# One score table with a running maximum over the level in place of masked scores per group, a rebuilt prologue and new engine lists, in a one-core transformer block

## What is computed

```python
levels = _compute_levels(token_ids, NUM_LEVELS)      # scan: clip(lvl + d, 0, 31)
h = level_emb[levels] * SCALE
h = h + attn(layernorm(h))      # 16 query heads, 4 key/value heads, head size 16, softmax over the 128 keys
h = h + ffn(layernorm(h))       # ternary weights W1, W2; relu(x @ W1.T + b1) @ W2.T + b2, 1024 hidden units
# _quantize(W): gamma = mean(|W|); clip(round(W / (gamma + 1e-5)), -1, 1)
```

## Time and profile before

| what | value |
|---|---|
| median of 3 runs | 60.76 us |
| lowest and highest | 60.25 and 62.35 us |
| span of the profiled execution | 59.6 us, the only time the profile gives for it |
| mean granted TensorE clock | 0.927 |
| busy: PE, PEld, DVE, ACT, POOL | 51.9, 40.2, 46.7, 37.6, 19.0 us |

### The profile page before, as it was taken

One profiled execution on the slowest core, in us unless ns is written; L12 is line 12 of the kernel. 1 busy time (PEld: TensorE's weight loads), 2 busy tenths in 40 slices (PEclk: granted clock), 3 DMA queues, 4 the chain that ended last, 5 costly groups with the idle time before them and its releaser, 6 DMA issues.

```text
span 59.6 us, 1125 instructions
## 1 busy us (share of the span) xinstructions
PE 51.9 (87%) x358; PEld 40.2 (68%) x358; DVE 46.7 (78%) x140; ACT 37.6 (63%) x99; POOL 19.0 (32%) x30
## 2 busy tenths in 40 slices
PE   2999999999999999989769999897999999996000
PEld 0333698555476997868448899596899989994000
DVE  1899795889999667469999999999998999427500
ACT  2726429960098876995999498697767599027400
POOL 6431000499999900000940009992000000000000
PEclk9999998555589999999999999999999999999985
DMA  0469799854100000000000000000000066700694
GB/s 0 85 195 202 225 396 415 302 151 122 50 0 5 0 0 0 16 0 0 0 0 0 0 0 0 11 0 0 0 0 0 0 207 228 259 19 1 214 346 144
DMA packets 4496, 5.36 MB, mean 90 GB/s; under 512 B 986, under 2 KB 3979, under 8 KB 4491
## 3 DMA queue, kind: packets, MB, share of 16 engines
q1 hardware_dynamic: 4458, 5.28, 27.3%
q10 hardware_dynamic: 32, 0.01, 0.1%
HBM read 3.19 MB, written 2.10 MB: 89 GB/s over the span
## 4 chain that ended last, share of the span: by engine, by line
PE 60%; DVE 23%; ACT 5%; issue 4%; DVEq 1%
PE psmisc L995 12%; PE psg L818 8%; PE pswt L974 7%; DVE tern L643 4%; DVE hl L712 4%; ACT cT L442 3%; DVE xn L697 3%; PE psg L871 3%; PE psg L873 3%; PE psg L903 3%; PE psg L872 3%; PE psg L895 3%; PE psg L918 2%; DVE hq L681 2%; DVE st L685 2%
## 5 line engine op out<-in xcount | busy, mean ns | idle before, releaser
L456 ACT ACTIVATE hr<-pswt,b1c 128x256 f32<-128x256 f32 x16 | 7.5, 476 | 2.7 <-PE pswt L974 2.2
L995 PE MATMUL psmisc<-w2T,hh 128*128 128x256 f32 x32 | 8.4, 291 | 0.3 <-DVE hl L712 0.3
L995 PE MATMUL psmisc<-w2T,hl 128*128 128x256 f32 x32 | 8.1, 282 | 0.0
L712 DVE TENSOR_TENSOR hl<-hr,hh 128x256 fp32r<-128x256 f32 x16 | 7.7, 509 | 0.3
L364 POOL TENSOR_SCALAR sg<-w 128x1024 bf16<-128x1024 f32 x2 | 7.2, 3628 | 0.0
L974 PE MATMUL pswt<-xhi,w1T 128*128 128x256 f32 x32 | 7.0, 299 | 0.0
L995 PEld LDWEIGHTS psmisc<-w2T,hh 128*128 128x128 f32 x32 | 6.1, 189 | 0.7 <-DVE hl L712 0.5
L974 PE MATMUL pswt<-xlo,w1T 128*128 128x256 f32 x32 | 6.4, 280 | 0.0
L995 PEld LDWEIGHTS psmisc<-w2T,hl 128*128 128x128 f32 x32 | 6.1, 190 | 0.0
L818 PE MATMUL psg<-warm 128*128 128x512 bf16 x11 | 5.1, 629 | 1.2 <-DVE tiny L540 1.2
L643 DVE SCALAR_TENSOR_TENSOR tern<-aw,thr,sg 128x512 bf16<-128x512 f32 x8 | 5.6, 739 | 0.0
(11 more groups left out here) (152 smaller groups left out, 124.4 us busy)
## 6 DMA issues: line engine op xcount, KB each, us to landing
w<-in_L_ffn_W_dram SPq DMA_DIRECT2D x4, 512.0 KB, 6.1
out_dram<-aw SPq DMA_DIRECT2D x8, 256.0 KB, 2.6
wq<-in_L_attn_Wq_dram SPq DMA_DIRECT2D x1, 256.0 KB, 2.8
wo<-in_L_attn_Wo_dram SPq DMA_DIRECT2D x4, 64.0 KB
emb<-in_L_tok_level_emb_dram SPq DMA_DIRECT2D x1, 128.0 KB
bo_bc<-in_L_attn_bo_dram SPq DMA_DIRECT2D x1, 128.0 KB, 7.6
b_bc<-in_L_ffn_b_dram SPq DMA_DIRECT2D x1, 128.0 KB, 6.2
wk<-in_L_attn_Wk_dram SPq DMA_DIRECT2D x1, 64.0 KB, 2.0
```

Source lines behind the costliest of these rows:

```text
L456: nc.scalar.activation(hr[:, n % NHR, :], pswt[n % 2][:, 0:RH], ACT.Relu, bias=b1c[:, j:j + 1]).then_inc(a_hr, 1)
L712: V.tensor_tensor(hl[:, n, :], hr[:, n % NHR, :], hh[:, n, :].bitcast(F32), ALU.subtract).then_inc(v_hl, 1)
L995: ins = mm(psmisc[r][:, 0:D], part[:, n, r * P:(r + 1) * P], w2T[:, j, :], start=(g < HALF and j == 0 and m == 0), stop=(j == FC - 1 and m ...
```

## The change

What it does, part by part:

- Scores are made once for all sequences: `scores()` is two matmuls of 128 columns with no mask (query rows on partitions, 4 key heads by 32 levels). The levels that a sequence has are a gapless range from 0 or from 1 up to its highest. Two DVE scans (`prefix_max`) give the running maximum along the level, one starting at level 0, one at level 1; `prefix_t`, `prefix_out` transpose and copy them; `level_ends`, `end_codes`, `end_columns` find the highest and lowest level of each sequence, `top_onehot` makes a one-hot of it, and the matmuls `maxima()` pick for each sequence the running maximum at its highest level. `max_hi`, `max_parts` split it into `ms`, and one `less_max()` of 16 matmuls on 32 partitions each serves all four groups, with one semaphore for all. `neg` and its matmul, the four reductions, `mxr` and `max_t` are gone.
- The prologue is rebuilt. The token DMA brings three copies of the tokens, so that one compare each handles the three opening and the three closing brackets, and a matmul (`drops`) adds them up; the scan then reads PSUM. Queries are made on 128 output partitions (4 matmuls in place of 8), the bias matmuls go first, ACT takes the high parts of the queries, POOL makes one half of `wqh`, `xT4`, `rep` and `sel`. `warm_up` is 5, 2 and 2 in place of 10 and 1.
- The signs of W1 go from ACT to DVE (1024 elements in each of two instructions). The copies into `cT` are shared: per group two on ACT and two on DVE. `magnitudes(1, 1)` goes ahead of the exponentials, and `table_bias` ahead of `threshold(0)`.
- All four lists are in a new order.

The diff, cut to its core:

```diff
+            act.dma_start(tok3[:], x.unsqueeze(0).to_broadcast([3, B, S])).then_inc(d_tok, 16)
...
             def exps(g, b):
-                act.wait_ge(p_et, g + 1)
                 if g == 0 and b == 0:
-                    act.wait_ge(v_cpos, 2)
+                    act.wait_ge(p_et, 1)
+                    act.wait_ge(v_cpos, 1)
...
             def ctx_out(g):
                 act.wait_ge(p_cT, g + 1)
-                for c in range(2):
-                    src = psg[g][64 * c:64 * c + 64, 0:D].rearrange("p (b a e l) -> p a e b l", b=2, a=2, e=H2)
-                    for a in range(2):
-                        dst = cT[64 * a:64 * a + 64, g].rearrange("p e (b c) l -> p c e b l", c=2)
-                        nc.scalar.activation(dst[:, c], src[:, a], ACT.Copy).then_inc(a_cT, 1)
+                for a in range(2):
+                    src, dst = ctx_halves(g, 0, a)
+                    ins = nc.scalar.activation(dst, src, ACT.Copy)
+                ins.then_inc(a_cT, 1)
...
+            query_hi(0)
+            query_hi(1)
             magnitudes(0, 0)
             magnitudes(0, 1)
-            signs(0)
+            prefix_out()
             magnitudes(1, 0)
-            max_out(0)
-            signs(1)
-            max_out(1)
-            max_out(2)
+            max_hi()
+            magnitudes(1, 1)
             exps(0, 0)
...
+            dve.wait_ge(c_opc, 6)
+            V.tensor_scalar(opened[:], tok3[:], opc[:, 0:1], None, ALU.is_equal).then_inc(v_cmp, 1)
             dve.wait_ge(v_st1, 1)
...
+            V.scalar_tensor_tensor(drop[:].rearrange("b (s e) -> b s e", e=2)[:, :, 0], tok3[:], opc[:, 1:2], opened[:],
+                                   ALU.is_equal, ALU.subtract).then_inc(v_drop, 1)
...
+            def level_ends():
+                dve.wait_ge(v_lev, 1)
+                V.tensor_reduce(ends[:, 0:1], levels, AX_X, ALU.max).then_inc(v_ends, 1)
+                V.tensor_reduce(ends[:, 1:2], levels, AX_X, ALU.min).then_inc(v_ends, 1)
+
+            def end_codes():
+                dve.wait_ge(v_ends, 2)
+                for i in range(2):
+                    V.scalar_tensor_tensor(ends[:, 2 + i:3 + i], ends[:, 1:2], (64.0, -64.0)[i], ends[:, 0:1],
+                                           ALU.mult, ALU.add).then_inc(v_code, 1)
+
+            def end_columns():
+                dve.wait_ge(c_sele, 1)
+                for i in range(2):
+                    dve.wait_ge(v_code, i + 1)
+                    V.tensor_scalar(endx[:, i, :], sele[:], ends[:, 2 + i:3 + i], None, ALU.mult).then_inc(v_endx, 1)
...
+            def top_onehot(i):
+                dve.wait_ge(p_ends, 1)
+                dve.wait_ge(c_row, 1)
+                V.scalar_tensor_tensor(top[:, i, :].rearrange("p (n k) -> p n k", k=KV),
+                                       pswt[1][:, i * P:(i + 1) * P].rearrange("p (n k) -> p n k", k=KV),
+                                       pnum[:, 0:1] if i == 0 else pm64[:, 0:1], bm[:].unsqueeze(1).to_broadcast([P, P // KV, KV]),
+                                       ALU.is_equal, ALU.mult).then_inc(v_top, 1)
+
+            def prefix_max(i):
+                dve.wait_ge(p_s, 1)
+                dve.wait_ge(c_reset, 3)
+                V.tensor_tensor_scan(pmx[:, i, :], reset[:, i, :], psmisc[1][:, 0:P], ABSENT, ALU.add, ALU.max).then_inc(v_pmx, 1)
...
+            def max_parts():
+                dve.wait_ge(c_row, 2)
+                dve.wait_ge(a_mhi, 1)
+                V.scalar_tensor_tensor(ms[:], mhi[:].bitcast(F32), lowrow[:, 0:1], psmisc[1][:, 0:P], ALU.mult, ALU.add).then_inc(v_ms, 1)
+
+            def signs(i):
+                dve.wait_ge(d_w1[i], 16)
+                V.tensor_scalar(sg[:, 0, i * 1024:(i + 1) * 1024], halves(0, i), 0.0, 0.5, ALU.is_ge, ALU.subtract).then_inc(v_sgn, 1)
...
-
-            def maxima(g):
-                dve.wait_ge(p_s, g + 1)
-                V.tensor_reduce(mx[:, g, :], psg[g][:, :].rearrange("p (n l) -> p n l", l=L), AX_X, ALU.max).then_inc(v_mx, 1)
...
+            def ctx_out(g):
+                dve.wait_ge(p_cT, g + 1)
+                for a in range(2):
+                    src, dst = ctx_halves(g, 1, a)
+                    ins = V.tensor_copy(dst, src)
+                ins.then_inc(v_cT, 1)
...
+            absent()
+            values()
+            table_bias()
             threshold(0)
-            maxima_hi(3)
```

PE's side of it (its list stands above):

```diff
+            def drops():
+                pe.wait_ge(v_drop, 1)
+                pe.wait_ge(c_seld, 1)
+                mm(pswt[1][0:B, 0:2 * S], seld[:], drop[:], start=True, stop=True).then_inc(p_drop, 1)
...
-            def less_max(g):
-                pe.wait_ge(a_ms, g + 1)
-                if g == 0:
-                    pe.wait_ge(c_sel, 2)
+            def less_max():
+                pe.wait_ge(v_ms, 1)
+                pe.wait_ge(c_sel, 1)
                 for b in range(BG):
-                    ins = mm(psg[g][:, b * P:(b + 1) * P], sel4[:, b * P:(b + 1) * P], ms[:, g, :], start=False, stop=True,
-                             skip_group_check=True)
+                    for g in range(NG):
+                        q = slice(L * g, L * (g + 1))
+                        ins = mm(psg[g][:, b * P:(b + 1) * P], sel[q, b * P:(b + 1) * P], ms[q, :], start=False, stop=True,
+                                 skip_group_check=True)
```

More of the change, by code:

```diff
@@ L220, in level_tower @@
         v_klo = sem("v_klo")
[L221 to L222 removed]
+        a_qhi = sem("a_qhi")
+        v_qlo = sem("v_qlo")
         v_vo = sem("v_vo")
@@ L752, in _ @@
             normalise(1)
+            ctx_out(0)
             ternary(0, 3)
-            inverse_sums(2)
-            table_bias()
-            normalise(2)
+            ctx_out(1)
             add_table(0)
@@ L844, in _ @@
-            pe.wait_ge(a_wqh, KC)
-            for h in range(G):
-                for k in range(KC):
-                    mm(psg[3][0:64, h * L:(h + 1) * L], wqh[:, k, h], xT1[:, k, 0:L], start=(h == 0 and k == 0), stop=False,
-                       skip_group_check=True)
-            pe.wait_ge(a_bqr, 1)
-            for h in range(G):
-                ins = mm(psg[3][0:64, h * L:(h + 1) * L], bqr[:, h], ones[0:1, 0:L], start=False, stop=True, skip_group_check=True)
-            ins.then_inc(p_q, 1)
@@ new lines, in query_bias, with levels_out @@
+            def query_bias():
+                pe.wait_ge(a_bqr, 1)
+                for a in range(2):
+                    mm(psg[3][:, a * L:(a + 1) * L], bqr[:, a], ones[0:1, 0:L], start=(a == 0), stop=False, skip_group_check=True)
+            def levels_out():
+                pe.wait_ge(v_lev, 1)
+                pe.wait_ge(c_selb, 1)
+                levels = lev[:].rearrange("b (s e) -> b s e", e=2)[:, :, 1]
+                for g in range(NG):
+                    ins = mm(pswt[0][:, g * S:(g + 1) * S], selb[:, g * P:(g + 1) * P], levels, start=True, stop=True)
+                ins.then_inc(p_lev, 1)
@@ new lines, in keys, with queries @@
+            def keys():
+                pe.wait_ge(a_xT1, 1)
+                pe.wait_ge(a_wk, 1)
+                for k in range(KC):
+                    ins = mm(psmisc[1][:, 0:L], wk[:, k].rearrange("p r n -> p (r n)"), xT1[:, k, :], start=False, stop=(k == KC - 1))
+                ins.then_inc(p_k, 1)
+            def queries():
+                pe.wait_ge(a_xT1, 1)
+                pe.wait_ge(a_wqh, 1)
+                pe.wait_ge(g_wqh, 1)
+                for a in range(2):
+                    for k in range(KC):
+                        ins = mm(psg[3][:, a * L:(a + 1) * L], wqh[:, k, a, :], xT1[:, k, :], start=False, stop=(k == KC - 1),
+                                 skip_group_check=True)
+                ins.then_inc(p_q, 1)
@@ new lines, in level_ends, with values @@
+            def level_ends():
+                pe.wait_ge(v_endx, 2)
+                pe.wait_ge(c_ones, 2)
+                mm(pswt[1][:, 0:2 * P], ones16[:], endx[:].rearrange("p i n -> p (i n)"), start=True, stop=True).then_inc(p_ends, 1)
+            def values():
+                pe.wait_ge(v_oh, 2)
+                pe.wait_ge(d_bv, 16)
+                mm(pswt[0][:, 0:KVD], ones[0:1, :], bvr[:], start=True, stop=False)
+                pe.wait_ge(d_wv, 16)
+                pe.wait_ge(g_xT4, 1)
+                for k in range(KC):
+                    mm(pswt[0][:, 0:KVD], xT4[:, k].rearrange("p b l -> p (b l)"), wv[:, k, :], start=False, stop=(k == KC - 1))
@@ new lines, in prefix_t, with maxima @@
+            def prefix_t():
+                for i in range(2):
+                    pe.wait_ge(v_pmx, i + 1)
+                    ins = nc.tensor.transpose(psmisc[0][:, i * P:(i + 1) * P], pmx[:, i, :], identf[:])
+                ins.then_inc(p_pmT, 1)
+            def maxima():
+                pe.wait_ge(a_pmT, 1)
+                pe.wait_ge(v_top, 2)
+                for i in range(2):
+                    ins = mm(psmisc[1][:, 0:P], top[:, i, :], pmT[:, i, :], start=(i == 0), stop=(i == 1))
```

(20 more changed lines are left out.)

627 lines of the change are left out of this document (325 added, 302 removed).

## The result

The changed kernel takes 67.78 us (median of four executions, 67.30 to 69.10) against 60.52 for the kernel before on the same chip (60.25 to 62.35); the ratio is 1.119, 95% interval 1.107 to 1.131. The forecast was 59.5, its range ended at 62.8, and the direction is wrong as well. The profiled execution took 67.94 us, its span is 65.5.

The account below looks back on a forecast made before the run. It took DVE, handing over with ACT, to have little room after a prologue to 18.35, and PE to bound from 41.8; -0.1 - 1.0 - 1.2 + 2.1 - 1.2 = -1.4, less 0.2, gave 59.5 us against 60.76, range 57.0 to 62.8.

Parts of the forecast that it names:

- Prologue, predicted -0.1: Up to the exponentials: PE at the lower clock needs 11.3 us behind xT1, exponentials at 18.2 against 18.35.
- rival 1: Prologue: warm-ups bring the full clock by about 6 and short matmuls hold it, 57.5 us; chance 0.30.
- the limit I named for a fast prologue: Prologue: with table_bias ahead of threshold(0), DVE waits for bo_bc until 16.1; no cost in the forecast itself.
- Other things in this stage are hidden: Prologue: POOL's new copies and selectors (4.4 to about 9), DVE's identities and the bo_bc wait cost nothing.
- My last sentence on what could go wrong: Closing caveat: an untimed wait, above all POOL's sel before less_max or sg before the ternaries of W2.
- The first term: Attention: context(0) starts at 19.3 in place of 20.3, once four exponentials are through; -1.0 us.
- The second term: Attention: sharing cT copies between ACT and DVE saves 0.6 us for each of the first two groups; -1.2.
- rival 2: Attention: clock at 1.2 GHz from 18 to the first long out_proj or ffn1 run, about +3.3, 62.8 us; chance 0.23.
- The window of rival 2: Attention: a granted clock under about 0.75 in 18 to 27 us would decide for rival 2.
- Hand-over, predicted +2.1: Second to fourth x_lo: DVE's new list takes 11.1 to 11.3 us, before 9.1; fourth x_lo at 41.7.
- Rival 3: Hand-over: DVE has 1.5 us more than taken, so the gain is given back, 60.7 us; chance 0.12.
- Last stretch, predicted -1.2: Behind the fourth x_lo, PE-bound: 13 ffn2 calls stand ahead of ffn1(1, 0), before 8; five at 0.24 us.

Follow-up runs that it names:

- e1: The changed kernel plus 11 dummy matmuls where PE waits, from the exponentials to the third group; 67.29 us, ratio 1.086 to the kernel before.
- e5: e4 plus 11 dummy matmuls where PE waits in the attention; 64.15 and 64.39 us undisturbed, 65.60 median.
- e6: e5 with all four cT copies of a group on ScalarE; 64.35 and 64.45 us undisturbed, ratio 1.060.
- e10: e6 with the signs of W2 made by VectorE instead of GpSimd, ahead of threshold(0); 62.57 us, ratio 1.027.
- e13: e10 with ten warm-up matmuls in a row at the start in place of five; 61.41 us in one undisturbed execution, median 63.51.
- e15: e13 with table_bias back in the attention, one W2 sign operation earlier, no warm-ups ahead of the scores; 60.61 and 60.89 us undisturbed, median 63.29.
- e11: The kernel before with GpSimd's list as in the change, so both W2 sign operations come later; 62.71 us, ratio 1.030.
- e8: The kernel before with only the shared cT copies, two of four per group on VectorE; 61.87 and 62.31 us undisturbed, ratio 1.022.
- e12: e10 without the 11 dummy matmuls; 64.26 us, ratio 1.054.
- e4: The changed kernel up to less_max, then the old order on PE, ACT and DVE, shared cT copies kept; 66.87 us, ratio 1.091.
- e7: e1 with the order of before from the first ffn1 on, spread(1, *) side by side; 64.96 us undisturbed, 66.50 median.
- e2: The changed kernel with the four spread(1, b) calls in a row; 66.82 us median, 65.15 in one undisturbed execution.

## Why the prediction was wrong, step by step

The runs form a ladder, by undisturbed executions: the change 67.6; with the clock held (e1) 66.3; with the old order too (e5) 64.3; copies back on ScalarE (e6) 64.4; signs off GpSimd (e10) 62.6; the kernel before 61.0. That is 1.3 + 2.0 - 0.1 + 1.8 + 1.6 = 6.6 us. Most rungs come from different chips. By the ratios to the kernel before, which ran beside each (60.4 undisturbed beside the change, 61.1 beside e1), the same steps are 2.0 + 1.7 - 0.1 + 2.0 + 1.6 = 7.2, so a single step may be off by 0.3, the first by 0.7. The order in which parts are undone matters too: the signs give 1.8 in the old order, 0.8 to 1.4 on one execution in the new one. The last 1.6 is not taken apart further than by e13 and e15.

**Prologue, predicted -0.1, measured +0.9.** The clock was called right (the lower level to the end), which rules rival 1 out. Two terms were mis-sized. PE was through with the transposes of `xT1` at 6.2, where I had the copy ready at 5.8; and PE needed 12.4 us behind them, not 11.3: the four matmuls of the query bias, 0.85 us [L952 in the chain], were in no term. The 22 passes took the 5.3 us that they were priced at. `less_max` was 0.6, not 1.0. That nothing waits for `bo_bc` held, and e13 shows the limit I named for a fast prologue: DVE waits until 17.2.

**"Other things in this stage are hidden": the step that failed unseen.** It priced GpSimd's new copies and not the rest of GpSimd's list. The value copies wait for DVE's `values`, which moved 6 us back, and the first sign operation of W2 went with them; the second was moved by hand, and its new place was not priced either. My last sentence on what could go wrong named `sg` before the ternaries of W2, without a time or a chance. e10 and e11 price it at 1.7 to 1.8 us in the old order, from both sides.

**Attention, predicted -1.0 and -1.2, measured +0.2.** The first term held in part. Six exponentials take 1.66 us from 19.27, so the fourth is through at 20.4, and `context(0)` follows at 20.55: 1.3 us behind the first exponential, where it was 2.0 before. That is -0.7; it doesn't show in the start of `context(0)`, because the prologue ends late. What `abs_total(1)`, which stands ahead of it in PE's list and waits for DVE's `thr`, costs it is 0.15 at the most. My sum also books the prologue's -0.1 twice, as 19.3 already holds it. The second term, -1.2, is the one that failed: from the first `context` to the second `x_lo` it is 13.2 us where it was 12.3. The copies were costed by what they take from ACT, and not by what they put into DVE's list: e8 shows +1.0 to +1.3. The stretch holds besides one ternary of 1.50, `rs` at 1.17 in place of 0.74, and the low clock, of which rival 2 spoke. With the clock held (e1) the new attention takes 13.7 us from the first exponential, 0.6 less than before, so a gain was there. The window of rival 2, here 19.3 to 29.3, has 0.76 and 0.89, just above the 0.75 from which it was to decide. The mechanism of rival 2 is real and mis-sized: 1.3 to 2.0 us (e1) or 1.7 (e12) against the 3.3 given. That PE's waits hide the rest fits, but no run separates it.

**Hand-over, predicted +2.1, measured +4.2.** Behind the attention, which missed by 2.4, this is the largest miss, 2.1, and the mechanism was right: DVE is the bound, busy 12.29 of 13.2 us. I had 11.2. The rest are the copies at 1.23 for 0.8, `norm_rows` at 1.56 for 1.2, the ternaries at 0.7, and 0.9 us of idle time; 0.45 of that is one wait for `out_proj(2)`, which PE brings late at 0.66 of its clock (1.71 us for four passes in the chain). With the clock held it is still 12.6 (e1), with the old order 9.3 (e4, e5): the order carries it, the attention's share of it included (e7). I had counted all eight `hidden_lo(0, *)` ahead of `x_lo(2)`, at 4.5 us, but not asked whether they have to be there: PE's long last stretch starts only behind DVE work that DVE could do beside it, as it does with three of them in the old order. Rival 3 had named this place, at 1.5 us, and its `norm_rows` under POOL at 0.8 is what came.

**Last stretch, predicted -1.2, measured +0.6.** Fewer `ffn2` calls are worth most of what I said: 106 matmuls in the window where the earlier trace rows has 117, and in e2 the stretch is 13.2 against 14.1, so -0.9. What I didn't price is where `spread(1, *)` went. Four pairs alone between other matmuls cost 1.7 us, side by side 0.44, and that ate the gain.

Nor did I see how little the score table brings by itself: with the rest put back and ten warm-ups the first exponential is at 17.96 (e13) or 18.53 (e15) against 18.35, and the best total equals the kernel before.

## What to carry to other kernels

When an edit moves one operation, follow every queue behind its consumers, the quiet engines' too: here a value matrix that became ready 6 us later dragged one GpSimd operation onto VectorE's ternaries, and a second was put there by hand. Both together cost 1.7 to 1.8 us in the old order (e10, e11). Work shifted from one engine to another has to be costed in the receiving engine's list, at the very place where it lands, and a gain of "done earlier" only counts ahead of the stretch that the same engine bounds. Keep matmuls on few partitions in groups; scattered one by one between full ones they cost four times as much here (1.7 us against 0.44).

## What the runs showed that I had not expected

- A GpSimd operation of 3.64 us does not slow VectorE throughout: the ternary that meets its start takes 1.50 in place of 0.74 us, the ones behind it 0.66 to 0.75, and GpSimd takes 3.64 as ever. It need not be a ternary: in e4 a 128x1 operation (`thr`) meets the start and takes 0.66 in place of 0.16, and all ternaries stay at 0.75; in the kernel before a 128x16 subtraction that takes 0.18 elsewhere takes 0.97 where GpSimd's second sign operation starts. In the other direction, GpSimd's value copies take 3.43 us in place of 2.54 beside VectorE's sign operations (e10). The Trainium skill, in "SBUF — State Buffer", section "SBUF: two separate sides", says in my words that the port pair of the two engines is an exclusive lock, held for a whole instruction. By that rule a ternary that starts 0.1 us behind the GpSimd operation would wait about 3.6 us for it, an estimate from the page's rule and the row's length; the rows show 0.76 more, and they decide.
- A pair of matmuls on 32 partitions takes 0.42 us alone and 0.11 when four pairs stand together. "TensorEngine Tiling (Array Packing)", Key Properties, in the Trainium skill says that changing the tiling mode drains TensorE; the rows agree, if that drain is what the lone pairs pay, which no run separates.
- The clock column reads 1.00 where nothing is recorded: in the first 18 us the spacing of 512-column matmuls (0.43) tells the level, the column doesn't.
- PE was busy in 17.54 of the first 19.3 us and still at 1.2 GHz; with ten warm-ups in a row the profiled executions of e13 and e15 had it up early, and others of the same kernels, of which there is no trace, took 1.9 us or more longer. Why is open.
